# v projected token-major from the second group on, another VectorE order, and the first group's k and ring loads moved

## What is computed

```python
xn = layernorm(x)                                  # x: 4 x 1024 x 1024, float32
q = heads((xn @ Wq + bq) * hd ** -0.5)             # 16 heads of 64
k = heads(xn @ Wk + bk)
v = heads(xn @ Wv + bv)
D = where(i >= j, exp(decay[h] * (i - j)), 0)
ret = einsum('bhid,bhjd->bhij', q, k) * D
ret = ret / clip(abs(ret.sum(-1)), 1, None)
attn = einsum('bhij,bhjd->bhid', ret, v)
g = group_norm(attn) * gn_w + gn_b                 # over each head's 64
ffn = nvfp4(xn) @ nvfp4(weight).T * scale + bias   # blocks of 16, 4-bit values
out = x + (silu(xn @ Wg + bg) * g) @ Wo + bo + ffn
```

## Time and profile before

| | |
|---|---|
| median of 3 runs | 2137.29 us (2134.43 to 2142.41) |
| the profiled execution | 2142.48 us, its span 2140.7 us |
| PE busy | 2080.3 us, 97% of the span |
| DVE busy | 1541.7 us, 72% |
| ACT, POOL busy | 685.9 us, 640.0 us |
| granted TensorE clock, mean | 0.991 of full |
| DMA | 275.61 MB, 129 GB/s |

### The profile page before, as it was taken

The page is one execution under the profiler, slowest core; times in us unless marked ns, Lnnn a source line. Parts: engine busy times, 40 slices in busy tenths (PEclk is TensorE's granted clock), DMA queues, the critical chain, the costliest instruction groups (busy, mean ns, idle before and its releaser), DMA issues.

```text
span 2140.7 us, 51098 instructions
## 1 busy us (share of the span) xinstructions
PE 2080.3 (97%) x18098; PEld 1053.5 (49%) x18098; DVE 1541.7 (72%) x4375; ACT 685.9 (32%) x1318; POOL 640.0 (30%) x456
## 2 busy tenths in 40 slices
PE   5988899999999999999999999999999999999999
PEld 3444444455455454555555555454555454555444
DVE  7899898988889877566767556767656767656732
ACT  5756623332223233322323322323322322322300
POOL 1323232332233333223332223233223233223220
PEclk8999999999999999999999999999999999999999
DMA  8878634334343443323333323333323333223343
GB/s 317 282 253 265 218 98 138 108 109 136 100 127 108 137 128 94 102 83 109 124 103 93 103 84 109 122 103 94 103 85 107 122 103 95 103 86 106 122 153 117
DMA packets 181686, 275.61 MB, mean 129 GB/s; under 512 B 117344, under 2 KB 117472, under 8 KB 181344
## 3 DMA queue, kind: packets, MB, share of 16 engines
q1 hardware_dynamic: 181600, 274.48, 39.8%
HBM read 204.18 MB, written 40.89 MB: 114 GB/s over the span
## 4 chain that ended last, share of the span: by engine, by line
PE 86%; DVE 11%; DMA 2%; issue 1%; ACT 0%; SPq 0%; DVEq 0%; ACTq 0%
PE mm L1288 54%; PE mm L1223 10%; PE tp L1223 6%; PE mm L1232 4%; PE tp L1298 3%; PE four L1338 3%; PE four L1351 2%; PE tp L1326 1%; PE four L1311 1%; PE four L1232 1%; PE tp L1251 1%; DVE wo L929 1%; DMA res<-in_w_f 1%; DMA parts<-wo 1%; DVE state L1041 1%
## 5 line engine op out<-in xcount | busy, mean ns | idle before, releaser
L1288 PE MATMUL mm<-xnT,wring 128*128 128x512 f16 x6144 | 1365.8, 381 | 13.8 <-DVE wring L929 6.8
L1288 PEld LDWEIGHTS mm<-xnT,wring 128*128 128x128 f16 x6144 | 598.2, 98 | 710.3 <-issue 25.2
L695 ACT ACTIVATE work<-four,gs 128x64 f32<-128x64 f32 x512 | 158.1, 414 | 554.2 <-DVE gs L1068 554.2
L556 POOL TENSOR_TENSOR yT<-gn,gate 128x512 f32 (+1 forms) x64 | 84.2, 1315 | 800.6 <-ACT gn L706 800.6
L1223 PE MATMUL mm<-wo,yT 128*128 128x512 f16 x960 | 214.1, 380 | 0.1
L1055 DVE BATCH_NORM_STATS2 gst<-four 128x6 f32<-128x64 f32 x512 | 73.5, 216 | 195.0 <-PE four L1351 194.8
L539 POOL TENSOR_TENSOR qparts<-qT,qparts 128x512 f16<-128x512 f32 x64 | 77.0, 1203 | 363.2 <-ACT qT L664 363.1
L539 POOL TENSOR_TENSOR kparts<-kT,kparts 128x512 f16<-128x512 f32 x64 | 84.2, 1316 | 225.1 <-ACT kT L664 225.1
L1223 PEld LDWEIGHTS mm<-wo,yT 128*128 (+1 forms) x960 | 91.0, 98 | 108.3 <-issue 0.2
L1223 PE MATMUL tp<-wo,yT 128*128 128x512 f16 x576 | 128.2, 379 | 0.0
L662 ACT ACTIVATE qparts<-mm,consts,down 128x512 f16<-128x512 f32 x64 | 49.7, 776 | 213.2 <-PE mm L1288 213.2
(11 more groups left out here) (198 smaller groups left out, 2648.8 us busy)
## 6 DMA issues: line engine op xcount, KB each, us to landing
wring<-parts SPq DMA_DIRECT2D x252, 512.0 KB, 3.9
xt<-in_x SPq DMA_DIRECT2D x34, 512.0 KB, 3.6
out<-res SPq DMA_DIRECT2D x32, 512.0 KB, 3.0
parts<-wo SPq DMA_DIRECT2D x28, 512.0 KB, 5.6
res<-in_x SPq DMA_DIRECT2D x28, 512.0 KB, 3.5
ftile<-in_w_f SPq DMA_DIRECT2D x12, 512.0 KB, 4.4
parts<-wring SPq DMA_DIRECT2D x8, 512.0 KB, 6.8
probs<-in_x SPq DMA_DIRECT2D x5, 512.0 KB, 4.6
```

The source lines that it names most:

```text
L556: nc.gpsimd.tensor_tensor(hi, gn[:], gate[:, u], ALU.mult)
L695: last = nc.scalar.activation(work[:, c * P + h * HD:c * P + (h + 1) * HD], ao[h][:, c * VW:c * VW + HD], ACT.Identity, bias=gs[:, 1, g:g ...
L1288: last = MM(mm[n % 2][:], wring[:, n, wj, k, :], xnT[:, parity, xj, k, :], start=(j == 0), stop=(j == 3 * KT - 1))
```

## The change

From SECOND on v is projected by `project_v(j)`, for both pairs of a body at once and token-major: the 128 tokens of x are stationary, and 256 weight columns (v of both pairs, in ring slots 1 and 3) move. Two calls, 48 matmuls of 256 columns each, replace two projections of 24 matmuls of 512, and the eight v transposes and `copy_v` go. `evacuate_v` writes v1, now four heads wide, and POOL adds the bias (`bias_v`, twice per body). Since slots 1 and 3 hold v first, g of both pairs is loaded into them after `project_v(1)` (`load_gates`), and v of the next body after the g projections.

VectorE: in FIRST the second half of x is quantized behind `split_lo` instead of ahead of `mask_scores(0)`, and `find_f_max` later. In MIDDLE `mask_scores(0)` comes ahead of the second half. In SECOND and THIRD both halves of the weight's quantizing move one place back.

FIRST: PE projects k of the next body's first pair between `scores(1)` and `state_increments(1)`, ACT empties it ahead of `normalize(1)`, the last `affine` of a body moves behind `x_hi` and `evacuate(0, 2)` of the next, and `load_slice` copies from the staging area `wo` (SBUF to SBUF) instead of from DRAM; `square` therefore waits for the ring load that reads its slice. Core of the diff:

```diff
+    if phase == FIRST:
+        t0, t1 = ("k0", "u0", "v1", "u1", "g1"), ("v0", "k1", "g0")
+    else:
+        t0, t1 = ("k0", "u0", "u1", "g1"), ("k1", "g0")
     return {n: (0, i + 1) for i, n in enumerate(t0)} | {n: (1, i + 1) for i, n in enumerate(t1)}
...
+def g_use(phase, u):
+
+    return mm_use(u, 3) if phase == FIRST else 3 + u
...
-        vT = sb("vT", [P, GROUP])
+        v_bias = sb("v_bias", [P, E])
...
-        v1 = sb("v1", [P, CH, 2, VW])
+        v1 = sb("v1", [P, CH, 4, VW])
...
+        vT = xqf[:].bitcast(F32)
...
-                    if (phase, i, u) == (FIRST, 0, 0):
-                        sp.wait_ge(stored[n], 32)
-                        sp.wait_ge(lo_done, 4 + n + 1)
-                        src, dst = wo[:, :, 4 + n, :], wring[:, n].rearrange("p b k x -> p b (k x)")
+                    if phase == FIRST and (i, u) != (CH - 1, 1):
+                        b, c = i + u, 4 * (1 - u) + n
+                        if (i, u) == (0, 0):
+                            sp.wait_ge(stored[n], 32)
+                        sp.wait_ge(lo_done, SLICES * b + c + 1)
+                        src, dst = wo[:, :, c, :], wring[:, n].rearrange("p b k x -> p b (k x)")
                     else:
                         if phase == FIRST:
                             wait_stored(n, q * 2 + u + 1)
                         src = a["parts"][n, ds(q * 2 + u + 1, 1)].rearrange("a p n -> p (a n)")
+                        if (phase, i, u, n) == (FIRST, CH - 1, 1, 3):
+                            sp.wait_ge(wrap_stored, 16)
+                            src = a["parts"][1, PAIRS + 1]
                         dst = wring[:, n].rearrange("p a b c -> p (a b c)")
                     sp.dma_start(dst, src).then_inc(s["w_" + MATS[n]], 16)
 
...
+                def load_gates():
+
+                    w("mm1_full", 2)
+                    for u in range(2):
+                        load_ring(2 * u + 1, 3, q * 2 + u)
+
+                def load_v(u):
+
+                    w("mm1_full", g_use(phase, u))
+                    load_ring(2 * u + 1, 1, q * 2 + 2 + u)
...
                     else:
                         move_x_parts()
                         load_slice(0, 3)
+                    load_slice(1, 0)
+                    pass_on(i + 1, range(0, 1))
+                    load_slice(1, 1)
+                    pass_on(i + 1, range(1, 2))
                     w("xq_ready", 1)
                     move_x()
                     load_x(1)
-                    pass_on(i + 1, range(0, 2))
-                    load_slice(1, 0)
-                    load_slice(1, 1)
-                    pass_on(i + 1, range(2, 4))
                     load_slice(1, 2)
+                    pass_on(i + 1, range(2, 3))
                     load_slice(1, 3)
+                    pass_on(i + 1, range(3, 4))
                     pass_on(i + 1, range(4, 5))
                     load_fs(F_TILES[i][1])
+                    if i == 1:
+                        sp.wait_ge(stored[5], 16)
+                        sp.dma_start(a["parts"][1, PAIRS + 1], a["parts"][1, 1]).then_inc(wrap_stored, 16)
+                        sp.dma_start(v_bias[:], a["bv"]).then_inc(v_bias_in, 16)
                     return
...
-                for n in range(4):
-                    load_slice(0, n)
+                load_slice(0, 0)
+                load_slice(0, 2)
+                load_gates()
                 move_x_parts()
                 w("xq_ready", 1)
                 load_x(1)
-                for n in range(4):
-                    load_slice(1, n)
+                load_slice(1, 0)
+                load_v(0)
+                load_slice(1, 2)
+                load_v(1)
                 w("out_ready", 1)
...
+                def bias_v(j):
+
+                    w("mm1_free", j + 1)
+                    pool.sem_inc(pool_turn, 1)
+                    out = v1[:, 2 * j:2 * j + 2, :, 0:HD]
+                    rows = v_bias[:, ds(q * (2 * P), 2 * P)].rearrange("p (h d) -> p h d", d=HD)
+                    nc.gpsimd.tensor_tensor(out, out, rows.unsqueeze(1).broadcast_to([P, 2, 4, HD]), ALU.add)\
+                      .then_inc(s["v_ready"], 1)
...
-                    if b == 1 and c >= 4:
-                        act.wait_ge(s["w_" + MATS[c - 4]], 16)
+                    loads = 2 * b - 1 if c >= 4 else 2 * b - 2
+                    if loads > 0:
+                        act.wait_ge(s["w_" + MATS[c % 4]], 16 * loads)
...
+                def evacuate_v(j):
+
+                    w("within", 0)
+                    w("mm1_full", j + 1)
+                    act.sem_inc(act_turn, 1)
+                    for u in range(2):
+                        from_u = mm[1][:].rearrange("p (c a h d) -> p c a h d", c=2, a=2, d=HD)[:, :, u]
+                        last = nc.scalar.activation(v1[:, 2 * j:2 * j + 2, 2 * u:2 * u + 2, 0:HD], from_u,
+                                                    ACT.Copy, scale=down[:, 1, pair(u)])
+                    last.then_inc(s["mm1_free"], 1)
...
                 evacuate(0, 0)
-                evacuate(0, 1)
+                evacuate_v(0)
                 affine(1, 1)
                 x_hi()
                 evacuate(0, 2)
-                copy_v(0)
                 decay_k(0)
+                evacuate_v(1)
+                evacuate(1, 0)
                 evacuate(0, 3)
-                evacuate(1, 0)
-                evacuate(1, 1)
                 decay_k(1)
                 evacuate(1, 2)
-                copy_v(1)
                 normalize(0)
                 evacuate(1, 3)
                 affine(0)
@@ -734,13 +803,15 @@
             def first_group(evacuate, affine, x_hi, copy_v, decay_k, normalize, i):
 
...
-                evacuate(0, 0)
+                if i == 0:
+                    evacuate(0, 0)
                 evacuate(0, 1)
                 if i:
-                    affine(1, 1)
                     square(i + 1, range(0, 4))
                 x_hi()
                 evacuate(0, 2)
+                if i:
+                    affine(1, 1)
                 copy_v(0)
                 decay_k(0)
                 if i:
...
+                if i + 1 < CH:
+                    evacuate(0, 0, ahead=1)
...
-                    if i:
-                        quantize_half(xt, 1)
                     mask_scores(0)
                     if i == 0:
                         quantize_half(xt, 1)
                     scale_batch()
...
-                    find_f_max(F_TILES[i][0])
+                    if i:
+                        quantize_half(xt, 1)
                     group_norm(0)
                     mask_scores(1)
+                    find_f_max(F_TILES[i][0])
                     split_lo(i + 1, range(2, 3))
...
                 quantize_half(xt, 0)
-                quantize_half(xt, 1)
+                if phase in QUANTIZE:
+                    quantize_half(xt, 1)
                 mask_scores(0)
                 if phase in QUANTIZE:
                     f_scales()
+                else:
+                    quantize_half(xt, 1)
                 states(0)
-                if phase in QUANTIZE:
-                    f_half(0)
                 group_norm(0)
                 mask_scores(1)
                 if phase in QUANTIZE:
-                    f_half(1)
+                    f_half(0)
                 states(1)
                 emit_half(w, 0, "mm0", 5)
                 if phase == MIDDLE:
                     emit_linear(w, 0, "mm1", 5, "mm0", 5)
+                else:
+                    f_half(1)
                 group_norm(1)
                 if phase in QUANTIZE:
                     emit_half(w, 1, "mm1", 5)
                     emit_done(w, "mm1_free", 5)
                 if phase == MIDDLE:
-                    emit_half(w, 1, "t1", 4)
...
+                def project_v(j):
+
+                    if j == 0:
+                        w("w_v", 0)
+                        w("w_g", 0)
+                    w("mm1_free", j)
+                    out = mm[1][:].rearrange("p (c a x) -> p c a x", c=2, a=2)
+                    for c in range(2):
+                        tokens = slice((2 * j + c) * P, (2 * j + c + 1) * P)
+                        n = 0
+                        for k in range(KT):
+                            for wj, xj in ((0, 0), (1, 0), (0, 1)):
+                                last = MM(out[:, c], xnT[:, parity, xj, k, tokens], wring[:, 1::2, wj, k, :],
+                                          start=(n == 0), stop=(n == 3 * KT - 1))
+                                n += 1
+                    last.then_inc(s["mm1_full"], 1)
...
                 if phase == FIRST and i == 0:
                     pe.wait_ge(sums_read, 1)
                     sum_slices(0, 4, 4)
-                project(0, 1)
-                if phase != FIRST or i:
+                if phase == FIRST:
+                    project(0, 1)
+                else:
+                    project_v(0)
+                if phase != FIRST:
```

(33 more changed lines are left out.)

71 lines of the change are left out of this document (45 added, 26 removed), and 4 rows, old and new, of the table PER.

## The result

The changed kernel takes 2194.9 us (median of 4 runs, 2192.2 to 2198.7) against 2136.7 for the kernel before: a ratio of 1.026, 95% interval 1.024 to 1.028. It is slower, and near the 2189 that was forecast. Its profiled execution took 2194.3 us.

A forecast was written before the change was run, and what follows sets the result against it. PE was taken to bound MIDDLE, and waits between PE and DVE to matter in the first group. First group +48, SECOND and THIRD +19, MIDDLE -15 gave +52: 2189 us, range 2155 to 2215.

The forecast's parts named there:

- v, the matmuls and transposes: Each body from SECOND on: 48 more matmuls +0.12 us, eight v transposes dropped -0.87; -0.75 where PE bounds, MIDDLE -15 us.
- Rival 3: Projections of v: short matmuls pay for their weight loads, 25 ns each, +67 us on the forecast, 2256 us; chance 0.05.
- rival 4: Ring loads of g arrive late, 1 us in each of 28 bodies, 2217 us; chance 0.05.
- `bias_v` at 0: POOL's bias adds stand beside 5 us projections and cost nothing while that cover holds; at worst +34 us.
- VectorE's order there, +19 with v's gain in it: SECOND and THIRD: PE's second projection waits for `emit_half(1)`, +2.4 us per body, 8 bodies, +19 us.
- First group, slot 3 at 41 us: Bodies 1 to 3: last square waits for slot 3's late ring load, increments start 13.6 us later each, 41 us.
- The sum of +48: First group in all: 41 us for slot 3's load, +4 for x's second half, +3 for k's early projection; range 33 to 62.
- the signs: First-group bodies 1 to 3: square idle some 14 us, PE idle 6 or more, projection near 8, bodies 73 to 77.
- Half 1 behind, +4: First group: DVE does the second half of x later, +2 us net in each of bodies 1 and 2.
- k ahead, +3: First group: k's projection one body early delays `state_increments(1)`, +3 us after body 0, 0 in later bodies.
- Rivals 1, 2 and 5: Slot 3's load no stall, 2112 us, 0.10; only the first group stalls, 2164, 0.13; small net stall, 2130 to 2145, 0.07.

The follow-up runs named there:

- v alone: Changed kernel with the first group and the VectorE order of SECOND and THIRD as before, v token-major and MIDDLE's changed order kept: 2131.6 us, ratio 0.9961.
- v without its bias: As v alone, but the bias of v is not added from the second group on, POOL only counts the semaphore: 2121.4 us, ratio 0.9913.

## Why the prediction was right, and where not

The whole, by the runs: first group +49 us, VectorE's order in the second and third groups +16 (2146.1 to 2131.6, ratios 1.0034 and 0.9961), v token-major with MIDDLE's order -8. Together +56 (1.0262; the rounded terms give 57); forecast +52. The terms are steps of one way back, so they must add up; a second way to the VectorE order, taken out of the changed kernel by itself, gives 16 too.

The traces divide it the same way. From the layernorm in SECOND's first body to the one in MIDDLE's first body, the kernel before takes 489.2 us, the changed one 512.2, v alone 496.7, and v without its bias 486.5. Nineteen MIDDLE bodies take 1217.9 us before and 1202.3 to 1202.4 in every version with v token-major, wherever its bias is added and even without it. So the bias costs time in the second and third groups only. Where the first group is left as before, SECOND's first layernorm starts anywhere from 275.0 to 279.9 us in six traces, so a few us there tell nothing.

That the total came within 4 us of the forecast is in part luck: the sum for the second and third groups lacked the bias and the slow projections, and part of their price was met by a wait at g's transposes that went away.

- *v, the matmuls and transposes.* Right: a MIDDLE body is 0.82 us shorter (0.75), 48 matmuls of 256 columns take 5.24 us to the transposes behind them, 109.2 ns each, and no gate load was waited for. Nothing of a weight load's 98 ns row shows in that pace. Rival 3 and rival 4 are out. Against the Trainium skill (TensorE: Matmul & The Clock Gate, Back-to-back issue gap) the measurement decides: nothing of the 25 ns more per matmul, estimated from its figures for 128 columns, shows at 256.
- *`bias_v` at 0.* Wrong in the second and third groups, the step that failed most clearly: "costs nothing while that cover holds". The cover was PE's; what it cost was VectorE's time, 2.7 us a body. Of that 1.2 us reached the period (62.0 against 60.8), and 10 us the kernel. I had read POOL as an engine with room and not looked at what runs beside its instructions on VectorE.
- *VectorE's order there, +19 with v's gain in it.* The wait was near what was worked out (2.7 us in SECOND and 1.9 in THIRD, 2.3 in the mean, against 4.17 - 1.46 - 0.31 = 2.4). The predicted period of 63.5 us was met in neither: 65.1 and 62.6. Order and v together cost 16 + 8 x 0.87 = 23 us there (61.2 to 62.0 us a body is v with its bias). Two things were not in the sum: the bias, and the slow `project_v(0)` behind the four waits of SECOND, 1.7 us each. Against them stands that the new order does away with the wait at g's transposes: 10.4 us in sum with the old order, 0.9 with the new.
- *First group, slot 3 at 41 us.* The sum of +48 is right (49), its division is not. By the trace the increments start 34.0, 35.3 and 34.7 us behind the layernorm, 10.1 to 12.4 later than before, not 13.6: the load was issued at 21.7 us, landed 3.2 us later, not 5, and the projection took 7.0, not 8.2. By the runs slot 3's place in the queue is 27 of it, when it is undone first. The other 13 are the affine behind x_hi, which I had counted only as a link of POOL's chain; that k's transposes wait for the same bank, 10.4 us, was not in the working. So the signs were met in part: PE's idle time ahead of the sums was 4.0 us (5.5 at most), not 6 or more, the square idled 10.9 us, not 14, and the bodies from layernorm to layernorm took 73.3, 75.8 and 69.1 us, not 73 to 77.
- *Half 1 behind, +4, and k ahead, +3.* Together 9 by the runs, with what is left of the squares' waits: 7 without the early projection, so 2 for it in this company. "In the later ones DVE is behind PE by then, 0" fits the changed kernel, where no more than 5 us show; in the version with the first group of before the early projection costs 20.
- *Rivals 1, 2 and 5* are out: the square idled 10.9 us, `emit_half(1)` was waited for in 8 places, and the first group cost 49 us, where rival 5 had some 5 us a body.

## To carry to other kernels

When a step is moved, list every resource that it holds and who waits for each: here one affine held a PSUM bank, and a load stood behind transposes in a queue with which it has nothing to do. An engine with a load of 33% (POOL from 340 to 760 us, before) isn't free if its instructions stretch those of the engine that sets the pace; price new POOL work by the longer VectorE instructions beside it. Undo the parts both alone and in pairs: the early projection cost 5 us or less in company and 20 alone.

## What the runs showed of the hardware

VectorE and POOL get in each other's way. A VectorE TENSOR_TENSOR of 128x512 takes 0.69 us with POOL idle, 2.50 beside x_lo, which takes 2.57 on POOL, and 1.55 and 1.65 beside POOL operations of 1.62 and 1.16 us; even in the kernel before, half 0 of x takes 9.0 us to quantize in the body that begins at 462.68, and half 1, with POOL idle, 4.3. In v alone the long ones shown end at 486.02, 487.61 and 492.13 us, each 0.54 or 0.55 us behind the end of the POOL operation that it ran beside (485.47, 487.06 and 491.59), as if most of their 0.69 us of work began when POOL's had ended. The Trainium skill (SBUF — State Buffer, SBUF: two separate sides) says that the two share one pair of ports, taken by a VectorE operation with two inputs in SBUF, such as these, and held for a whole instruction, so that the other engine waits. The trace fits that in the constant 0.54 us; no run was made to tell it from other forms of sharing.

Behind SECOND's PE waits of 2.7 to 2.8 us the projection ran partly at the lower clock. The granted clock from 390.0 to 397.5 us is 0.77, and over the body from 455.34 us 0.97, where MIDDLE bodies without waits show 1.00; 48 matmuls took 6.9 us instead of 5.2. Behind THIRD's waits of 1.8 to 1.9 us the granted clock stayed at 1.00 (from 712.0 to 717.5 us) and the matmuls at 5.2 us.
